# Two transposed blocks of the next group issued between the query blocks of a decoder layer's output projection

## What is computed

```
y  = y + attn @ w_out.T + b_out                  # output projection and residual
yn = _ln(y, dec_n2_s, dec_n2_b)                  # layer norm over the 512 features
q  = yn @ wq.T + bq                              # queries of the cross-attention
```

## Time and profile before

| | |
|---|---|
| time, median of 3 runs | 2991.94 us (2988.29 to 2993.01) |
| the profiled execution | 2988.92 us, of which the span of its instructions 2987.1 us |
| PE busy | 2741.8 us (92%) |
| DVE, ACT, POOL busy | 1600.5, 1242.6, 380.7 us |
| the stage's steady slots | about 1737 to 1908 us of the span |

### The profile page before, as it was taken

The page is one execution under the profiler, slowest core; times in us unless marked ns, Lnnn a source line. Parts: engine busy times, 40 slices in busy tenths (PEclk is TensorE's granted clock), DMA queues, the critical chain, the costliest instruction groups (busy, mean ns, idle before and its releaser), DMA issues. The chain is left out here.

```text
span 2987.1 us, 40688 instructions
## 1 busy us (share of the span) xinstructions
PE 2741.8 (92%) x12704; PEld 1809.4 (61%) x12704; DVE 1600.5 (54%) x3867; ACT 1242.6 (42%) x2630; POOL 380.7 (13%) x470
## 2 busy tenths in 40 slices
PE   5789987999999999999999489779969999999998
PEld 4678873444444444444444277557747787777877
DVE  4244438777777777777776366467632221222211
ACT  0032221555555555555555244278823222332222
POOL 0300003000000000000000112177546000000000
PEclk7899996999999999999999799989979999999999
DMA  9344446222222222222220577455431000000000
GB/s 290 72 166 177 169 158 151 61 68 65 66 66 65 65 66 65 65 65 65 65 65 8 134 210 220 150 164 170 135 107 39 29 29 29 1 28 28 28 15 14
DMA packets 131907, 271.31 MB, mean 91 GB/s; under 512 B 31669, under 2 KB 52661, under 8 KB 126202
## 3 DMA queue, kind: packets, MB, share of 16 engines
q1 hardware_dynamic: 126490, 253.53, 28.9%
q0 software_dynamic: 5216, 15.33, 1.8%
HBM read 174.39 MB, written 99.98 MB: 92 GB/s over the span
## 5 line engine op out<-in xcount | busy, mean ns | idle before, releaser
L983 ACT ACTIVATE sa_pr<-sa_st 128x512 f32<-128x512 f32 (+3 forms) x1280 | 610.7, 532 | 557.1 <-DVE sa_st L1046 317.2
L951 PE MATMUL sa_ov<-sa_pr,sa_v 128*33 128x512 f32 (+3 forms) x2560 | 533.9, 538 | 0.0
L1032 DVE TENSOR_REDUCE sa_part<-sa_mp 128x1 f32<-128x512 f32 (+3 forms) x768 | 411.5, 582 | 114.0 <-PE sa_mp L932 113.5
L942 PE MATMUL sa_st<-sa_q,sa_k 97*128 97x512 f32 (+3 forms) x1280 | 440.9, 413 | 16.8 <-ACT sa_pr L983 13.7
L942 PEld LDWEIGHTS sa_st<-sa_q,sa_k 97*128 97x128 f32 x1280 | 216.5, 189 | 317.2 <-ACT sa_pr L983 213.7
L932 PE MATMUL sa_mp<-sa_k,sa_q 96*128 96x512 f32 (+3 forms) x1280 | 371.8, 385 | 24.9 <-DVE sa_mp L1010 19.2
L1627 PE MATMUL ff_o<-ff_w,ca_k 128*128 128x512 f32 x1536 | 374.6, 393 | 3.0 <-DVE ca_k L1682 3.0
L1029 DVE CUSTOM_DVE_ANT_0 sa_mp<-sa_mp,sa_ub 128x512 f32<-128x512 f32 (+3 forms) x512 | 317.3, 663 | 76.9 <-PE sa_mp L932 67.3
L1682 DVE TENSOR_TENSOR ca_k<-ca_v,ca_k 128x512 fp32r<-128x512 f32 x128 | 94.1, 735 | 474.6 <-ACT ca_k L1664 474.6
L105 PE MATMUL ff_f<-ff_ln_hi,ff_w 128*128 128x512 f32 x1024 | 345.4, 398 | 2.9 <-DVE ff_ln_lo L530 2.9
L1627 PEld LDWEIGHTS ff_o<-ff_w,ca_k 128*128 128x128 f32 x1536 | 287.2, 188 | 71.2 <-DVE ca_k L1682 3.4
(11 more groups left out here) (186 smaller groups left out, 3077.4 us busy)
## 6 DMA issues: line engine op xcount, KB each, us to landing
sa_q<-scratch_q SPq DMA_DIRECT2D x192, 128.0 KB, 4.6
sa_k<-scratch_k SPq DMA_DIRECT2D x192, 128.0 KB, 4.8
scratch_q<-qkv_qst SPq DMA_DIRECT2D x32, 512.0 KB, 2.8
scratch_k<-qkv_qst SPq DMA_DIRECT2D x32, 512.0 KB, 2.8
scratch_q<-sao_qst SPq DMA_DIRECT2D x32, 512.0 KB, 2.8
ca_q<-scratch_q SPq DMA_DIRECT2D x32, 512.0 KB, 4.1
scratch_v<-qkv_vst SPq DMA_DIRECT2D x8, 1056.0 KB, 5.2
sa_v<-scratch_v SPq DMA_DIRECT2D x16, 528.0 KB, 7.4
```

Source lines behind the costliest of these rows:

```text
L942: pe.matmul(st[bank(u, h)][:, 0:w], ks[n.par][:, h, kb * P:(kb + 1) * P], qs[n.par][:, h, g * GW + c0:(g + 1) * GW], start=True, stop=True ...
L951: last = pe.matmul(ov[64 * h:64 * h + VW, c0:GW], vs[n.par][:, kb, h, :], pr[:, u % 4, h, 0:GW - c0], start=(u in opens), stop=(u in ends))
L983: act.activation(pr[:, u % 4, h, 0:w], st[bank(u, h)][:, 0:w], ACT.Exp, scale=SCALE).then_inc(s["exp"], 1)
L1032: dve.tensor_reduce(to, tile, AX_X, ALU.max).then_inc(s["red"], 1)
```

## The change

In the slots that have a successor, transposed block 0 of group g + 1 is now issued ahead of the third query block (m = 2), transposed block 1 ahead of the fourth (m = 3), and blocks 2 and 3 stay behind it. `transpose` waits for `normed` where its list begins with block 0, so that this wait moves along.

```
                     norm.wait_ready(pe, g)
                     for m in range(KC):
+                        if m >= 2 and left:
+                            norm.transpose(pe, g + 1, (m - 2,))
                         waits(pe, sq["ev"], KC * g + m)
                         cols = slice(m * P, (m + 1) * P)
                         product(pe, qps[m % 2][:], [((wq[0][:, c, cols], wq[1][:, c, cols]), norm.pair(g.par, c))
                                                     for c in range(KC)]).then_inc(sq["mm"], 1)
                     if left:
-                        norm.transpose(pe, g + 1)
+                        norm.transpose(pe, g + 1, (2, 3))
```

## The result

| | before | changed |
|---|---|---|
| median of 22 runs each | 2991.68 us (2985.56 to 2994.99) | 2997.26 us (2989.87 to 2999.88) |
| ratio | | 1.002, 95% interval 1.0013 to 1.0026 |
| span of the profiled execution | 2987.1 us | 2992.5 us |

The changed kernel is slower by 5.6 us of the medians. The interval of the ratio makes it 3.9 to 7.8 us. The forecast was 4.0 us slower, 2995.9, with a range of 2990.5 to 3000.5.

A forecast was written before the change was run, and what follows sets the result against it. PE was taken to bound the kernel, with ACT pacing the tail. Block 1's 3.6 us plus block 0's 0.38 in slot 6 made 4.0 us slower: 2991.9 + 4.0 = 2995.9 us, range 2990.5 to 3000.5.

The forecast's parts named there:

- Block 0 in the hole costs nothing: Ahead of query block 2, PE's 1.19 us wait for DVE covers transposed block 0: 0 us in slots 0 to 5.
- Block 1 costs 0.515 us in each slot: Ahead of query block 3, PE has no wait to cover transposed block 1: 7 x 0.515 = 3.6 us.
- The tail gives nothing back: Between query block 3 and the next projection, ACT sets the pace: still 3.35 us despite 1.03 us less PE work.
- Slot 6, 0.90 us: Last slot with a successor: little DVE wait left, so block 0 costs 0.38 us, besides block 1's 0.515.
- The sum, 4.0 us: Whole kernel: 3.6 us for block 1, 0 for block 0 in slots 0 to 5, 0.38 in slot 6; slower.
- The price of a block: PE time per transposed block of four transposes: 0.515 us, from eight taking 1.03 us.
- The lower bound of the range: Four transposes before the projection's start took 0.41 us, the low price per block, giving 3.1 us in all.
- The rival of the clock: PE's clock falls in the emptier tail: 1.55 us a fall, 10.9 in all seven, the change then 14.9 slower; chance 0.08.

The follow-up runs named there:

- block 0 alone: Against the kernel before, only transposed block 0 moved, ahead of the third query block; blocks 1 to 3 stay behind the fourth: ratio 1.0005, median 2993.67 us.
- filler: Six unused 512-column matmuls added behind the fourth query block: ratio to before 1.0001 with transposed blocks 0 and 1 ahead of the third, 1.0014 on the changed kernel.
- both blocks in the hole: Against the kernel before, transposed blocks 0 and 1 both moved ahead of the third query block: ratio 1.0011, median 2992.97 us.
- both ahead of the fourth: Against the kernel before, transposed blocks 0 and 1 both moved ahead of the fourth query block: ratio 1.0021, median 2998.34 us.
- the old order in slot 6: The change in slots 0 to 5, PE's old order in slot 6, against the kernel before: ratio 1.0011, median 2995.18 us.

## Why the prediction was right, point by point

- *Block 0 in the hole costs nothing.* Shown by the run with block 0 alone: cycles as before. PE's wait there was 0.95 to 1.04 us by the profile's column and shrank to 0.51 to 0.60.
- *Block 1 costs 0.515 us in each slot.* Right in place, small in size: 162.25 - 159.28 = 2.97 us for six cycles, 0.50 each.
- *The tail gives nothing back.* Shown three ways: with the emptier tail ACT's rows keep their spacing, a filler of 1.4 us in it costs nothing, and the tail shrinks when ACT's order changes.
- *Slot 6, 0.90 us.* From its first query matmul to transposed block 2 it took 1908.70 - 1896.02 = 12.68 us before and 1914.49 - 1901.04 = 13.45 after: 0.77 us.
- *The sum, 4.0 us.* The terms measured give 2.97 + 0.77 = 3.7 us. The end adds 1.4 us in two of three profiles of the change, and nothing in the third; the sum of the forecast had no term for it, so that its 4.0 us lie near the measured 5.6 with about 1 us of clock missing, on the mean of the three. From slot 0's first query matmul to the last of the stage it is 5.1, 5.2 and 3.6 us more than in the mean of the two profiles before (189.66). The medians differ by 5.6; the rest is within the interval. The spans of single executions cannot settle such a sum: in the two profiles of before, slot 0's first query matmul starts at 1736.74 and 1741.55 us, and from the last query matmul to the end of the span it is 1060.8 and 1057.6 us. That the profiled spans differ by 5.4 us is in part chance: 2.05 us lie ahead of slot 0's first query matmul, 5.19 in the stretch to the stage's last, and -1.87 behind it.
- *The price of a block* was read wrongly, with little harm. I divided the length of eight transposes, 1.03 us, by two. But that length holds the whole length of the last one, 0.27 us, so the pace is (1.03 - 0.27) / 7 = 0.109 us from start to start and a block of four is 0.44. The 129 ns a transpose that the prediction names is the same misreading. From query block 2 to the end of query block 3 the change took 6.05 to 6.11 us in slots 0 to 5 where the kernel before took 5.57 to 5.60: 0.44 for the block, and the rest because some products behind it start 0.231 to 0.236 us apart instead of 0.227. The lower bound of the range, 0.41 from start to start, was the better row.
- *The rival of the clock*, at 0.08, was put too low. I argued that each tail has 3.35 us without a product in either order. But at the end of the stage the fall came earlier, before or within block 3, in all three profiles of the change and in neither of before, and recovery was late in two. The table says the same of slot 6 in the other kernels: block 3 took 0.96 to 1.12 us in the five profiles of the change and of both blocks in the hole, and 0.65 or 0.66 in the five with the old tail there or the filler, but also in the two of block 0 alone and of both ahead of the fourth. In the steady slots the order of the change had no fall in 24 tails (three profiles, and the one with the old order in slot 6), though the other orders with blocks taken out of the tail had them: 1 in 6, 4 in 12, 1 in 6. None was seen in the 12 tails of before and the 12 with a filler. That the emptier tail is the cause fits all of this, and the filler's block 3 (0.66 us in both profiles) speaks for it; but the falls are too few, and the times too close, to call it shown. Why the steady tails of the change were spared stays open. What pattern of work lets the clock fall was not tried.

## What to carry to other kernels

An idle time of PE belongs to whoever ends it. Work moved out of it gives nothing back when the releaser is another engine's list: find where that engine takes the moved block up, and move that place along with it. Here the same move on PE alone was 5.6 us slower, and with ACT and DVE following, 15 to 20 us faster. And read the price of an inserted block from start to start, not from a merged row's length.

## What was not expected of the hardware

The granted clock fell to 1.2 GHz within tails, or in the first matmuls behind them, in which PE stood still for no longer than 1.45 us at a time, with transposes and a wait of 0.67 us behind it, and once where the longest wait was 1.01 us. It did so in some executions and slots and not in others of the same instructions. A fall made a steady cycle 1.4 to 1.6 us longer, with matmuls of 512 columns 0.43 us from start to start instead of 0.23. With six matmuls of unused result in the wait, no tail of slots 0 to 5 grew and none of the twelve saw a fall; the fall in the last slot, behind a wait of 3.39 us, came all the same.
